# The last feed-forward block's second product as seven half-size products, with the residual transposed into the banks of two accumulators

## The chip, the cores and the metric

One NeuronCore of one Trainium2 chip runs the whole kernel in one launch. The time is that of the device, in microseconds, as the median of several executions. The engines are called PE (TensorE, with PEld for its weight loads), DVE (VectorE), ACT (ScalarE), POOL (GpSimd) and SP (SyncE, which here only issues transfers).

## What is computed

The reference is a decoder of two layers on x, float32, 2 x 2048 rows of 512: attention, cross attention, a feed-forward part of three residual blocks, then a long convolution, another cross attention and a mixture of experts. The change is in the feed-forward part, which for each of three blocks does this on the normalised x, with weights dequantised from integers:

```
h = x
for blk in range(3):
    i0, i1 = (2 * blk, 2 * blk + 1)
    y = _qlora_linear(h, qweights[i0], scales[i0], biases[i0], lora_a[i0], lora_b[i0])
    y = _layernorm(y, ln_gamma[blk], ln_beta[blk])
    y = jax.nn.gelu(y, approximate=False)
    y = _qlora_linear(y, qweights[i1], scales[i1], biases[i1], lora_a[i1], lora_b[i1])
    h = y + h
return h
```

and then adds the result to the x that came in.

## The kernel before, in words

The feed-forward stage (stage_ffn, L1240 to L1967) keeps h transposed in on-chip memory (hT, four tiles of 128 features by all 4096 rows). Rows are worked in chunks of 512 (eight chunks, NC; four tiles of 128 rows each, TJ). A step s is one chunk of one block, 24 in all; LAST is 16, the first step of the last block. A step has two units for the first product (FIRST) and two for the second, one unit for the row tiles tb and tb+2. The list `units` sets the order on PE and DVE: first product of step s+1, then second product of step s.

First products, and the second products of blocks 0 and 1 (SECOND), are Strassen-Winograd products: seven products of half size (`product`, L1810 to L1813: two matmuls of 128x256 each) in place of eight. Each needs sums of tiles: of rows (mix_rows on POOL, L1466 to L1480), of the hidden tiles after gelu (mix_hidden on POOL, L1482 to L1496), and of the weights (mix_first and mix_second on DVE). A unit uses three banks, a, b and e, in the order p1, p4 of the unit before, p2, p5, p6, p3, p7 (`fast`); DVE takes the results out piece by piece between them (`evict`, L1666 to L1692; c21 of a unit comes in the evict of the next one, after its first piece).

The second product of the last block (WHOLE) is done in full: for each tile of 128 rows four matmuls of 128x512 (L1945), and four of 128x128 with the identity as moving operand that add the transposed hT, the residual, into the same bank (L1947). DVE adds the bank to a tile of xn (L1703). That tile was filled by `base` on POOL (L1498 to L1505): x plus the last bias.

Queues around this. POOL's program, for each step s: mix_hidden(s) (only for s < LAST), rstd2 of step s+1, mix_rows of step s+2, and base of output chunk s+2-LAST. base(c+2) waits for the load of x (L1430) and for the store of chunk c (L1417), since it fills the same half of xn. SP's program, for each output chunk c: wait for the last eviction of the chunk, issue its store, in chunk 5 issue the early loads of the next stage (L1980 and L1981), then issue the load of x for chunk c+2. The last chunk is stored tile by tile (L1422). ACT turns the hidden tiles through gelu into gT (L1757) and normalises y (L1741); PE turns y for it (turn_g, L1799), for step s+1 inside the first unit of step s+2.

Of the kernel before, what the change touches and what calls it, by code (L numbers as in the profile page):

```python
# [1239 lines left out]
def stage_ffn(nc, st, nxt, x_in, x_out, bias, gamma, beta):  # L1240
# [7 lines left out]
    with st:  # L1248
# [50 lines left out]
        o_mm = st.sem("o_mm")  # L1299
        o_done = st.sem("o_done")  # L1300
# [4 lines left out]
        FIRST, SECOND, WHOLE = range(3)  # L1305
# [11 lines left out]
        fast_before = [sum(k != WHOLE for k, _, _ in units[:g]) for g in range(len(units) + 1)]  # L1317
        nth = lambda kind, s, tb: fast_before[unit_at[kind, s, tb]] + 1
# [3 lines left out]
        whole_part = lambda s, u: (s - LAST) * TJ + u + 1  # L1322
# [42 lines left out]
        def chunk_set(s):  # L1365

            n = nth(SECOND, s, 1)
            return [(c11_done, n), (c12_done, n), (c22_done, n), (c21_done, n)]

        @block.sync  # L1370
        def _(sp):
# [40 lines left out]
            for c in range(NC):  # L1412
                s = LAST + c
                if c < NC - 1:
                    sp.wait_ge(o_done, whole_part(s, TJ - 1))
                    st.plain(sp)
                    sp.dma_start(chunk_rows(x_out, c), xn[:, c % 2]).then_inc(stored[c % 2], 16)  # L1417
                else:
                    for u in range(TJ):
                        sp.wait_ge(o_done, whole_part(s, u))  # L1420
                        st.plain(sp)
# [13 lines left out]
        def _(pool):  # L1435
# [46 lines left out]
            def mix_hidden(s):  # L1482
# [28 lines left out]
            for s in range(-1, NS):  # L1511
                if 0 <= s < LAST:
# [17 lines left out]
        def _(dve):  # L1530
# [40 lines left out]

            def mix_second(b):
# [27 lines left out]
            def work(g, slot):  # L1600

                kind, s, tb = units[g]
                if kind == FIRST:
# [17 lines left out]
                    if tb == 1 and slot == 2:  # L1621
# [3 lines left out]
                        if s - 1 == NC:  # L1625
                            mix_second(1)
                else:
# [17 lines left out]
            def places(g):  # L1645

                kind, s, tb = units[g]
                if kind == FIRST:
                    return [y[:, tb + 2 * r, half_] for r in range(2) for half_ in (lo, hi)]
                first = rows(s).start  # L1650
                return [hT[:, tb + 2 * r, first + h * HW:first + (h + 1) * HW] for r in range(2) for h in range(2)]

            def plus_bias(g, dst, bank, right, lower):

                kind, s, tb = units[g]
                if kind == FIRST:
                    return dve.tensor_tensor(dst, bank, b0[:, s // NC, hi if right else lo], ALU.add)
                u = tb + 2 * lower
                return dve.scalar_tensor_tensor(dst, bank, b1c[:, s // NC, u:u + 1], dst, ALU.add, ALU.add)

            def c21(g):
                dve.wait_ge(p4_mm, fast_before[g] + 1)
                plus_bias(g, places(g)[2], ps[:, g % 2, 0:HW], 0, 1).then_inc(c21_done, 1)

            def evict(g):
                kind, s, tb = units[g]  # L1666
                n = fast_before[g] + 1
# [1918 lines left out]
```

## Time and profile before

| what | us |
|---|---|
| median of 3 runs | 5355.99 |
| all runs | 5347.31, 5355.99, 5356.1 |
| the profiled execution, its own time | 5345.93 |
| span of its first to last instruction | 5344.1 |
| the last block's second products, from 1611.95 to 1843.30 | 231.35 |
| mean granted TensorE clock, share of full | 0.98 |

In a timeline each row gives the start, how long it took, engine, line, operation, and what is written from what; x4 means that four instructions are merged. A float32 matmul is recorded as two. Matmul ends are modelled, so the time that a group costs PE is read from the distance between starts. What stands in brackets is idle time of the engine before it and what ended it.

### The profile page before, as it was taken

What the parts mean: (1) busy time and instruction counts of PE and PEld (TensorE: products, weight loads), DVE (VectorE), ACT (ScalarE), POOL (GpSimd) and SP (SyncE); (2) the same over time, 40 slices, a digit from 0 to 9 for tenths busy, and PEclk for the clock granted to TensorE, in tenths of its full rate; (3) what the DMA queues carried; (4) which work ended last, traced back from release to release, by engine and by line L of the source; (5) the groups of instructions that cost most, each with busy time, mean ns of one, the idle gap of its engine ahead of it and who ended that gap; (6) DMA issues with size and microseconds to landing.
All of it is one profiled execution on the core that took longest, in us unless ns stands there. A gap on an engine that the chain in (4) does not pass through costs nothing. (4 is left out here: it accounts for less than half of the span.)

```text
span 5344.1 us, 79687 instructions
## 1 busy us (share of the span) xinstructions
PE 5070.8 (95%) x26624; PEld 2763.8 (52%) x26624; DVE 2764.3 (52%) x4714; ACT 1732.0 (32%) x2238; POOL 1691.6 (32%) x1428
## 2 busy tenths in 40 slices
PE   9999989979999999899979999699999999999998
PEld 4444446668887566444444555534444444444444
DVE  4243237756663355355532565555555555555554
ACT  1011015534332200334321433134444444444433
POOL 1000005545553211000012222534444444444443
PEclk9999999989999999999999999899999999999999
DMA  1010021230012233799976022335546667889996
GB/s 58 8 48 8 11 83 53 65 97 32 24 32 63 101 107 132 171 219 216 221 198 226 24 72 77 100 105 150 179 143 189 211 216 250 267 288 332 383 383 235
DMA packets 493432, 771.88 MB, mean 144 GB/s; under 512 B 119505, under 2 KB 263638, under 8 KB 492708
## 3 DMA queue, kind: packets, MB, share of 16 engines
q1 hardware_dynamic: 377072, 723.32, 41.9%
q0 software_dynamic: 36160, 43.09, 4.1%
q10 hardware_dynamic: 79988, 2.67, 1.0%
q8 instruction: 129, 2.11, 0.2%
q14 instruction: 83, 0.68, 0.0%
HBM read 577.15 MB, written 116.26 MB: 130 GB/s over the span
## 5 line engine op out<-in xcount | busy, mean ns | idle before, releaser
L3467 PE MATMUL ex_ps<-ex_w,ex_xT 128*64 128x512 f32 x5248 | 1192.9, 596 | 13.3 <-DVE ex_w L3369 11.7
L3369 DVE COPY ex_w<-ex_shelf 128x4096 f32 x328 | 753.2, 2296 | 368.0 <-PE ex_ps L3467 243.4
L3418 ACT ACTIVATE ex_w<-ex_shelf 128x4096 f32 x164 | 593.4, 3618 | 888.3 <-PE ex_ps L3483 770.1
L3467 PEld LDWEIGHTS ex_ps<-ex_w,ex_xT 128*64 128x64 f32 x5248 | 366.4, 137 | 625.8 <-issue 589.0
L3483 PE MATMUL ex_ps<-ex_w,ex_hT 128*64 128x256 f32 x5248 | 596.8, 380 | 26.0 <-issue 22.1
L3315 POOL DMA_INDIRECT ex_x<-moe_xn,ex_ix x328 | 558.1, 1702 | 132.4 <-issue 99.0
L3332 POOL DMA_INDIRECT out<-ex_y,ex_ix_out x164 | 293.6, 1790 | 894.5 <-DVE ex_xT L3356 432.0
L3483 PEld LDWEIGHTS ex_ps<-ex_w,ex_hT 128*64 128x64 f32 x5248 | 383.9, 137 | 283.2 <-issue 119.7
L2759 POOL TENSOR_TENSOR go_xb<-go_xr,go_bias 128x2048 f32<-128x2048 f32 x8 | 38.2, 4775 | 719.0 <-DMA go_xr<-x 652.8
L3375 DVE TENSOR_TENSOR ex_h<-ex_g,ex_ps 128x512 f32<-128x512 f32 x164 | 112.5, 686 | 252.1 <-PE ex_ps L3467 214.3
L617 PE MATMUL at_ps<-at_xT,at_kT 128*128 128x512 f32 (+3 forms) x640 | 239.3, 529 | 1.6 <-ACT at_kT L511 1.6
L617 PEld LDWEIGHTS at_ps<-at_xT,at_kT 128*128 128x128 f32 x640 | 116.7, 190 | 121.8 <-issue 109.1
L1757 ACT ACTIVATE ff_gT<-ff_ps,ff_bet,ff_gam 128x128 f32<-128x128 f32 x384 | 137.5, 484 | 121.7 <-PE ff_ps L1799 121.6
L3423 ACT ACTIVATE ex_g<-ex_ps 128x512 f32<-128x512 f32 x164 | 98.0, 597 | 232.8 <-issue 232.8
L2624 PE MATMUL cv_ps<-cv_xin,cv_split 128*128 128x512 f32 x320 | 155.9, 626 | 17.7 <-ACT cv_g L2513 9.4
L2645 PE MATMUL cv_ps<-cv_gt,cv_fwd 128*64 128x256 f32 x1280 | 157.0, 388 | 9.3 <-DMA cv_gt<-cv_g 9.3
L1741 ACT ACTIVATE ff_y<-ff_y,ff_nm,ff_rs 128x512 f32<-128x512 f32 x96 | 72.8, 807 | 272.2 <-POOL ff_nm L1461 272.2
L2580 DVE TENSOR_TENSOR cv_m<-cv_z,cv_hat 128x512 f32<-128x512 f32 x128 | 79.8, 685 | 150.0 <-ACT cv_z L2538 149.5
L891 POOL TENSOR_TENSOR xb_s<-xb_s,xb_rec 128x616 f32<-128x616 f32 x64 | 78.0, 1218 | 233.1 <-DVE xb_rec L961 232.1
L575 PE MATMUL at_ps<-at_v,at_low 128*128 128x512 f32 x336 | 146.8, 592 | 0.0
L2513 ACT ACTIVATE cv_g<-cv_ps 128x512 f32<-128x512 f32 x160 | 94.7, 599 | 136.8 <-PE cv_ps L2624 136.7
L2191 PE MATMUL pr_ps<-pr_t,pr_s 128*128 128x384 f32 x384 | 135.9, 487 | 3.2 <-DVE pr_t L2114 1.4
(360 smaller groups left out, 8130.6 us busy)
## 6 DMA issues: line engine op xcount, KB each, us to landing
ex_shelf<-L_ffn_w SPq DMA_DIRECT2D x128, 2048.0 KB, 17.0
ex_shelf<-L_ffn_wo SPq DMA_DIRECT2D x64, 2048.0 KB
cv_gt<-cv_g SPq DMA_DIRECT2D x320, 128.0 KB, 3.7
cv_vt<-cv_v SPq DMA_DIRECT2D x256, 128.0 KB, 5.2
ff_x<-x SPq DMA_DIRECT2D x16, 1024.0 KB, 7.5
ex_raw_x<-slot_token ACTq DMA_DIRECT2D x656, 0.5 KB
at_low<-x SPq DMA_DIRECT2D x8, 1024.0 KB, 8.4
x<-at_acc SPq DMA_DIRECT2D x8, 1024.0 KB, 4.2
```

Source lines behind the costliest of these rows:

```text
L575: i = pe.matmul(ps[:, 4 + n % 4, :], prob[g][:, j % 4, (it - 4 * g) * P:(it - 4 * g + 1) * P], v[:, j, :], start=j == js[0], stop=j == js[-1])
L617: i = pe.matmul(ps[:, bank + ic - origin // CH, lo - ic * CH:], kT[:, k, j * P:(j + 1) * P], xT[:, k, lo:(ic + 1) * CH], start=k == 0, sto ...
L1757: i = act.activation(gT[:, k, j * P:(j + 1) * P], ps[:, side_bank(("g", s, j)), k * P:(k + 1) * P], ACT.Gelu, bias=bet[:, b, k:k + 1], sca ...
L2191: i = pe.matmul(bank[:, 0:NPC], lhs[:, k], rhs[:, k], start=first and k == 0, stop=k == HK - 1, skip_group_check=not first)
L2624: i = pe.matmul(bank, split[:, u // 4, :], rows, start=True, stop=True)
L2645: i = pe.matmul(ps[o * RT:(o + 1) * RT, z_bank(n, q) + ri, u * CW:(u + 1) * CW], fwd[:, r, ri, :], gt[:, n % 2, r, :], start=True, stop=True)
L3315: pool.indirect_dma_start(out=x[:, p, h, :], out_offset=None, in_=xn_q, in_offset=bass.IndirectOffsetOnAxis(ap=ix[:, p, h:h + 1], axis=0)) ...
L3332: pool.indirect_dma_start(out=out_q, out_offset=bass.IndirectOffsetOnAxis(ap=ix_out[:, p:p + 1], axis=0), in_=y[:, p, :], in_offset=None, ...
L3369: dve.tensor_copy(w_s[n][:, :], pick(shelf[n], buf)).then_inc(w_set[n].sem, 1)
L3418: act.activation(w_s[2][:, :], pick(shelf[2], buf), ACT.Copy).then_inc(w_set[2].sem, 1)
L3467: mm = pe.matmul(ps[q * G:(q + 1) * G, which, 0:FQ], xT[:, p % 2, k, :], wu[which][:, k, q * FQ:(q + 1) * FQ], start=k == 0, stop=k == KD - 1)
L3483: mm = pe.matmul(ps[q * G:(q + 1) * G, 4, 0:DQ], hT[:, p % 2, k, :], wd[:, k, q * DQ:(q + 1) * DQ], start=k == 0, stop=k == FC - 1)
```

## The change

The units of the last block are of a new kind, THIRD, and run through `fast` and `evict` as the others do. WHOLE, its two functions and the semaphores o_mm and o_done go away, and so does the case distinction of three helpers that told when a bank is free. In place of weights as the stationary operand, gT is (the result has rows on the partitions). The diff, cut to its core:

```diff
-            units += [(SECOND if s < LAST else WHOLE, s, tb) for tb in range(2)]
+            units += [(SECOND if s < LAST else THIRD, s, tb) for tb in range(2)]
...
+        second = lambda s: SECOND if s < LAST else THIRD
...
-        def chunk_set(s):
+        def chunk_set(s, tb=1):
...
-            n = nth(SECOND, s, 1)
+            n = nth(second(s), s, tb)
             return [(c11_done, n), (c12_done, n), (c22_done, n), (c21_done, n)]
...
                 if c < NC - 1:
-                    sp.wait_ge(o_done, whole_part(s, TJ - 1))
-                    st.plain(sp)
+                    for done in chunk_set(s):
+                        sp.wait_ge(*done)
+                        st.plain(sp)
                     sp.dma_start(chunk_rows(x_out, c), xn[:, c % 2]).then_inc(stored[c % 2], 16)
                 else:
-                    for u in range(TJ):
+                    for u in TILES:
+                        for done in chunk_set(s, u % 2):
...
                 if s:
-                    pool.wait_ge(p4_mm, nth(SECOND, s - 1, 1))
+                    pool.wait_ge(p4_mm, nth(second(s - 1), s - 1, 1))
                 g11, g12, g21, g22 = gT[:, 0:HK, lo], gT[:, 0:HK, hi], gT[:, HK:KD, lo], gT[:, HK:KD, hi]
+                if s >= LAST:
+                    g21, g12 = g12, g21
+                    pool.tensor_tensor(g_t[:, X3], g11, g21, ALU.subtract).then_inc(g_t_done, 1)
+                    pool.wait_ge(g_t_done, n + 1)
+                    pool.tensor_tensor(g21, g21, g22, ALU.add).then_inc(g_t_done, 1)
+                    pool.wait_ge(g_t_done, n + 2)
+                    pool.tensor_tensor(g_t[:, X2], g21, g11, ALU.subtract).then_inc(g_t_done, 1)
+                    pool.wait_ge(g_t_done, n + 3)
+                    pool.tensor_tensor(g_t[:, X4], g12, g_t[:, X2], ALU.subtract).then_inc(g_t_done, 1)
+                    return
...
             for s in range(-1, NS):
-                if 0 <= s < LAST:
+                if s >= 0:
                     mix_hidden(s)
...
+            def mix_third():
+                b = NB - 1
+                v = w[:, b % 2, 1]
+                b11, b12, b21, b22 = v[:, 0:HK, lo], v[:, 0:HK, hi], v[:, HK:KD, lo], v[:, HK:KD, hi]
+                dve.wait_ge(w_done, KD * 2 * NB)
+                dve.wait_ge(p4_mm, nth(SECOND, LAST - 1, 1))
+                dve.tensor_tensor(w_s[:, X3], b22, b12, ALU.subtract).then_inc(w_s_done, 1)
...
                         if s - 1 == NC:
                             mix_second(1)
+                        if s - 1 == LAST:
+                            mix_third()
...
             def c21(g):
-                dve.wait_ge(p4_mm, fast_before[g] + 1)
+                dve.wait_ge(p4_mm, g + 1)
+                if units[g][0] == THIRD:
+                    dve.wait_ge(c11_done, g + 1)
                 plus_bias(g, places(g)[2], ps[:, g % 2, 0:HW], 0, 1).then_inc(c21_done, 1)
...
+                if kind == THIRD and tb == 0:
+                    dve.wait_ge(base_done, s - LAST + 1)
                 plus_bias(g, d11, a, 0, 0).then_inc(c11_set, 1)
-                if g and units[g - 1][0] != WHOLE:
+                if g:
                     c21(g - 1)
                 work(g, 0)
                 dve.wait_ge(p2_mm, n)
                 dve.wait_ge(c11_set, n)
-                dve.tensor_tensor(d11, b, d11, ALU.add).then_inc(c11_done, 1)
+                if kind == THIRD:
+                    both = xn[:, s % 2, tb::2, lo]
+                    dve.tensor_tensor(both, ps[:, 2 + g % 2, :].rearrange("p (r d) -> p r d", r=2), both, ALU.add).then_inc(c11_done, 1)
+                else:
+                    dve.tensor_tensor(d11, b, d11, ALU.add).then_inc(c11_done, 1)
...
+                if kind == THIRD:
+                    dve.wait_ge(c22_set, n)
+                    both = xn[:, s % 2, tb::2, hi]
+                    dve.tensor_tensor(both, ps[:, 4 + g % 2, :].rearrange("p (r d) -> p r d", r=2), both, ALU.add).then_inc(c12_done, 1)
+                    dve.wait_ge(c12_done, n)
...
-            def evict_whole(g):
...
+                if kind == THIRD:
+                    return {1: (gT[:, 0:HK, mine], v[:, 0:HK, lo]), 2: (gT[:, HK:KD, mine], v[:, HK:KD, lo]), 4: (gT[:, HK:KD, next_], w_s[:, X4]),
+                            5: (gT[:, 0:HK, next_], v[:, 0:HK, hi]), 6: (g_t[:, X2, :, mine], w_s[:, X2]),
+                            3: (g_t[:, X4, :, mine], v[:, HK:KD, hi]), 7: (g_t[:, X3, :, mine], w_s[:, X3])}
...
+            def residual(g, k, bank):
+
+                _, s, tb = units[g]
+                for q in range(TJ):
+                    i = pe.matmul(bank[:, q * P:(q + 1) * P], hT[:, k + q % HK, rows(s, tb + q // HK * 2)], ident[:, :],
+                                  start=q >= HK, stop=True, skip_group_check=True)
+                return i
...
-                if g and units[g - 1][0] != WHOLE:
+                if g and units[g] != (THIRD, NS - 1, 0):
                     p4(g - 1)
                 side_work(g, 0)
-                bank_b_free(g)
-                product(bb, *op[2], True).then_inc(p2_mm, 1)
-                bank_e_free(g)
+                if g >= 2:
+                    pe.wait_ge(c11_done, g - 1)
+                last = product(bb, *op[2], True)
+                if kind == THIRD:
+                    last = residual(g, 0, bb)
+                last.then_inc(p2_mm, 1)
...
                 side_work(g, 2)
                 if kind == FIRST:
                     pe.wait_ge(h_s_done, 4 * (2 * s + tb) + 3)
+                elif kind == THIRD and tb == 0:
+                    pe.wait_ge(g_t_done, 4 * s + 4)
                 pe.wait_ge(c22_set, n)
-                product(eb, *op[3], False).then_inc(p3_mm, 1)
+                last = product(eb, *op[3], False)
+                if kind == THIRD:
+                    last = residual(g, HK, eb)
+                last.then_inc(p3_mm, 1)
...
-            def whole(g):
...
-                if units[g][:2] == (WHOLE, NS - 1) and units[g][2] == 0:
+                if units[g] == (THIRD, NS - 1, 0):
+                    p4(g - 1)
                     for j in TILES:
                         turn_g(NS - 1, j)
-                if units[g][0] == WHOLE:
-                    whole(g)
-                else:
-                    fast(g)
+                fast(g)
+            p4(len(units) - 1)
```

Unchanged in `fast`, and reached by the new units: ahead of p5 the first unit of a step waits for the second operation of mix_hidden (g_t_done 4s+2), ahead of p6 for the third.

## Rows read from the trace of the kernel before

**Rows 1.** The page's first part: busy time of each engine.

```profile
PE 5070.8 (95%) x26624; PEld 2763.8 (52%) x26624; DVE 2764.3 (52%) x4714; ACT 1732.0 (32%) x2238; POOL 1691.6 (32%) x1428
```

**Rows 2.** Stretches: us, busy of PE, PEld, DVE, ACT, POOL, clock, DMA share, GB/s.

```profile
1611.95:1843.30 231.35, 226.57 (x965) 153.04 (x963) 77.64 (x173) 61.09 (x140) 80.66 (x110) 0.99 0.21 68
1661.27:1692.42 31.15, 31.15 (x139) 21.77 (x138) 11.51 (x26) 8.73 (x20) 12.99 (x18) 1.00 0.22 68
```

**Rows 3.** Timeline of PE, a second product of the last block and what follows.

```profile
1674.25 3.60 PE L1945 MATMUL ff_ps<-ff_w,ff_gT 128*128 128x512 f32 x8
1677.68 1.05 PE L1947 MATMUL ff_ps<-ff_ident,ff_hT 128*128 128x128 f32 x8
1678.57 1.03 PE L1812 MATMUL ff_ps<-ff_w_t,ff_hT 128*128 128x256 f32 x4
1679.44 3.60 PE L1945 MATMUL ff_ps<-ff_w,ff_gT 128*128 128x512 f32 x8
...
1691.53 1.05 PE L1947 MATMUL ff_ps<-ff_ident,ff_hT 128*128 128x128 f32 x8
1692.42 1.03 PE L1812 MATMUL ff_ps<-ff_w,ff_hT 128*128 128x256 f32 x4
```

**Rows 4.** Timeline, weight loads beside their matmuls, and a DVE eviction.

```profile
1701.73 0.84 PEld L1812 LDWEIGHTS ff_ps<-ff_w,ff_h_s 128*128 128x128 f32 x4
1701.94 1.03 PE L1812 MATMUL ff_ps<-ff_w,ff_h_s 128*128 128x256 f32 x4
...
1702.22 0.41 DVE L1679 TENSOR_TENSOR ff_y<-ff_ps,ff_y 128x256 f32<-128x256 f32 x1
```

**Rows 5.** Timeline of block 1 around the start of a first product.

```profile
1569.65 1.03 PE L1812 MATMUL ff_ps<-ff_w,ff_hT 128*128 128x256 f32 x4
...
1571.38 1.04 PE L1799 MATMUL ff_ps<-ff_ident,ff_y 128*128 128x128 f32 x8
...
1572.43 0.47 DVE L1659 SCALAR_TENSOR_TENSOR ff_hT<-ff_ps,ff_b1c,ff_hT 128x256 f32<-128x256 f32 x1
...
1577.78 1.27 POOL L1490 TENSOR_TENSOR ff_g_t<-ff_gT 128x512 f32<-128x512 f32 x1 [0.68 <-ACT ff_gT L1757]
...
1581.83 1.27 POOL L1496 TENSOR_TENSOR ff_g_t<-ff_gT,ff_g_t 128x512 f32<-128x512 f32 x1
```

**Rows 6.** Timelines of SP and POOL, last block: store, x load, base, twice.

```profile
1693.40 0.38 SPq L1417 DMA_DIRECT2D x<-ff_xn  x1
...
1693.88 0.44 SPq L1430 DMA_DIRECT2D ff_x<-x  x1
...
1702.07 4.52 POOL L1505 TENSOR_TENSOR ff_xn<-ff_x,ff_b 128x2048 f32<-128x2048 f32 x1 [8.62 <-DMA ff_x<-x]
...
1789.01 1.14 SPq L1430 DMA_DIRECT2D ff_x<-x  x1
...
1799.55 4.51 POOL L1505 TENSOR_TENSOR ff_xn<-ff_x,ff_b 128x2048 f32<-128x2048 f32 x1 [12.66 <-DMA ff_x<-x]
```

**Rows 7.** Timeline of PE in block 1, where DVE mixes its second weights.

```profile
1390.72 1.03 PE L1812 MATMUL ff_ps<-ff_gT,ff_w 128*128 128x256 f32 x4
...
1395.12 1.10 PE L1812 MATMUL ff_ps<-ff_gT,ff_w 128*128 128x256 f32 x4 [1.65 <-DVE ff_w_s L1584]
...
1397.07 1.13 PE L1812 MATMUL ff_ps<-ff_gT,ff_w_s 128*128 128x256 f32 x4
```

**Rows 8.** Timeline of the end of the stage, the last chunk.

```profile
1817.01 1.04 PE L1799 MATMUL ff_ps<-ff_ident,ff_y 128*128 128x128 f32 x8
...
1817.64 5.69 ACT L1757 ACTIVATE ff_gT<-ff_ps,ff_bet,ff_gam 128x128 f32<-128x128 f32 x16 [4.28 <-PE ff_ps L1799]
...
1823.39 5.35 PE L1945 MATMUL ff_ps<-ff_w,ff_gT 128*128 128x512 f32 x8 [2.07 <-ACT ff_gT L1757]
...
1842.65 0.69 DVE L1703 TENSOR_TENSOR ff_xn<-ff_ps,ff_xn 128x512 f32<-128x512 f32 x1 [3.64 <-PE ff_ps L1947]
```

**Rows 9.** The four microseconds inside that slow restart.

```profile
1825.00:1829.00 4.00, 4.00 (x11) 1.86 (x10) 0.00 (x0) 0.00 (x0) 0.00 (x0) 0.78 0.00 0
```

More of the change, by code:

```diff
@@ L1314, in stage_ffn @@
                 units += [(FIRST, s + 1, tb) for tb in range(2)]
-            units += [(SECOND if s < LAST else WHOLE, s, tb) for tb in range(2)]
+            units += [(SECOND if s < LAST else THIRD, s, tb) for tb in range(2)]
         unit_at = {u: g for g, u in enumerate(units)}
-        fast_before = [sum(k != WHOLE for k, _, _ in units[:g]) for g in range(len(units) + 1)]
-        nth = lambda kind, s, tb: fast_before[unit_at[kind, s, tb]] + 1
+        nth = lambda kind, s, tb: unit_at[kind, s, tb] + 1
+        second = lambda s: SECOND if s < LAST else THIRD
         part = lambda s, u: s * TJ + u + 1
         seq = lambda s, j: s * TJ + TILES.index(j) + 1
-        whole_part = lambda s, u: (s - LAST) * TJ + u + 1
         QUARTERS = [(b, i, k) for b in range(NB) for i in range(2) for k in range(KD)]
@@ L1649, in places @@
                     return [y[:, tb + 2 * r, half_] for r in range(2) for half_ in (lo, hi)]
+                if kind == THIRD:
+                    return [xn[:, s % 2, tb + 2 * r, half_] for r in range(2) for half_ in (lo, hi)]
                 first = rows(s).start
@@ L1657, in plus_bias @@
                     return dve.tensor_tensor(dst, bank, b0[:, s // NC, hi if right else lo], ALU.add)
+                if kind == THIRD:
+                    return dve.tensor_tensor(dst, bank, dst, ALU.add)
                 u = tb + 2 * lower
@@ L1687, in evict @@
                 dve.wait_ge(c12_set, n)
[L1688 removed]
+                if kind == THIRD:
[3 more added lines that the diff above has]
+                    dve.wait_ge(c12_done, n)
+                else:
+                    dve.tensor_tensor(d12, e, d12, ALU.add).then_inc(c12_done, 1)
                 dve.wait_ge(p7_mm, n)
@@ L1692, in evict @@
                 work(g, 2)
-            def evict_whole(g):
-                _, s, tb = units[g]
-                c = s - LAST
-                for i in range(2):
-                    u = 2 * tb + i
-                    dve.wait_ge(o_mm, whole_part(s, u))
-                    if u == 0:
-                        dve.wait_ge(base_done, c + 1)
-                    o = xn[:, c % 2, u, :]
-                    dve.tensor_tensor(o, ps[:, 2 * i + g % 2, :], o, ALU.add).then_inc(o_done, 1)
-                    if i == 0 and units[g - 1][0] != WHOLE:
-                        c21(g - 1)
-                    work(g, 2 * i)
             for j in range(TJ):
@@ L1720, in _ @@
             for g in range(len(units)):
-                if units[g][0] == WHOLE:
-                    evict_whole(g)
-                else:
-                    evict(g)
+                evict(g)
+            c21(len(units) - 1)
         @block.scalar
@@ L1931, in fast @@
                 product(ab, *op[7], False).then_inc(p7_mm, 1)
-            def whole(g):
-                _, s, tb = units[g]
-                b = s // NC
-                if tb == 0:
-                    pe.wait_ge(g_done, part(s, TJ - 1))
-                    if s % NC == 0:
-                        pe.wait_ge(w_done, KD * (2 * b + 2))
-                for i in range(2):
-                    u = 2 * tb + i
-                    bank = ps[:, 2 * i + g % 2, :]
-                    (bank_b_free if i else bank_a_free)(g)
-                    for k in range(KD):
-                        pe.matmul(bank, gT[:, k, u * P:(u + 1) * P], w[:, b % 2, 1, k, :], start=k == 0, stop=False)
-                    for k in range(KD):
-                        o = pe.matmul(bank[:, k * P:(k + 1) * P], hT[:, k, rows(s, u)], ident[:, :], start=False, stop=k == KD - 1)
-                    o.then_inc(o_mm, 1)
-                    if i == 0:
-                        if units[g - 1][0] != WHOLE:
-                            p4(g - 1)
-                        side_work(g, 0)
             for n in range(KD):
```

59 lines of the change are left out of this document (21 added, 38 removed).

## The prediction, made before any run of the changed kernel

> **What bounds the kernel now.** I read the page's busy line first: PE is busy 95% of the span, every other engine about half or less [rows 1]. The stretches come next. From the start of the last block's second products to their end, 231.35 us, PE is busy 226.57 of them, and in one whole chunk of 31.15 us it has no gap at all, while POOL is busy 12.99 and DVE 11.51 [rows 2]. So in this stage time is the number of passes that PE makes, and another engine counts only where PE waits for it.
>
> The timeline of PE gives the prices, as spacing of starts, since ends are modelled and overlap [rows 3]. A matmul of float32 is two records. Four matmuls of 128x512 last from 1674.25 to 1677.68, 3.435 us; the four 128x128 ones that add the residual 0.89; a half-size product (two of 128x256) 0.865. A tile of the old second product is thus 4.325 us, a chunk 17.3 us and 0.865 for the fourth product of the unit before, which sits in it. The first product's two units take 12.98, the 31.15 of a chunk less the 18.17 from 1674.25 to 1692.42.
>
> **PE's work.** Removed per chunk: 4 x 3.435 = 13.74 us. Added: 14 products x 0.865 = 12.11. The residual stays: four groups of four 128x128 matmuls, 4 x 0.89, since each of two accumulators takes the halves of two tiles. Net 1.63 us a chunk, 8 chunks: **-13.0 us**, if nothing waits. The p4 of a chunk's last unit moves 0.865 into the next chunk's first unit, which makes that pair 13.84 us long.
> In the trace the weight loads lie under the matmuls: four loads of 0.84 us in sum stand beside products that still follow each other every 0.865 us [rows 4]. So the greater number of loads is free.
> The Trainium skill (TensorE: Matmul & The Clock Gate, Part 3) says that a weight load overlaps running matmuls only where it targets another row group of the array; here all 128 rows are used, so by that rule the 24 added loads of a chunk, 107 ns each by its section on LDWEIGHTS, would cost 2.6 us, more than the gain. The trace contradicts it.
>
> **Evictions.** Two DVE operations of 128x512 per unit (0.69 us; a row of them comes with the tail) become two of that size and five of 128x256, 0.41 to 0.42 each [rows 4]; with the statistics some 5 us in a unit of 7.83. The last residual matmuls end 0.865 before p7, so the widened eviction is done before c22 can start, and c22 is done 1.5 us after those matmuls, where PE wants it at 2 x 0.865 = 1.73. Nothing, if PE is not late already; if DVE were more than 0.2 us slower, p4 would wait by the rest.
>
> **Where POOL puts the new mixing: the term that decides.** The mixing of the hidden tiles is four operations on POOL, 1.35 us apart, the last ending 5.32 after the first begins [rows 5]. It now runs in the last block too. POOL's program has, for chunk s: mixing, row statistics, row mixing, and then the base of output chunk s+2. That base is queued ahead of the next mixing. It waits for an x load, which SP issues behind the store of chunk s, which waits for that chunk's last eviction. In the trace, with T the start of the next first product (1692.42): store issued T+0.98, load T+1.46, base T+9.65 to T+14.17 [rows 6]. Today that costs nothing, as the base is wanted a chunk later.
> After the change the last eviction is the c21 behind p4. In block 1, where this order runs already, it starts at T+2.78 (T is 1569.65) behind the turns of the hidden tile [rows 5]; it ends near T+3.2, so store, load and base all come 2.3 us later. The base then runs from T+12.0 to T+16.5, and the mixing from T+16.5: second operation done at T+19.1, third T+20.5, fourth T+21.8.
> PE reaches the second product at T+13.84, and p5, which wants the second operation, at T+13.84 + 3 x 0.865 + 0.89 = T+17.3; p3, which wants the fourth, would start at T+19.05 and starts at T+21.97 with 0.15 us for the semaphore. **Stall 2.9 us**, in five chunks: **+14.6**.
> In the sixth chunk the next stage's early loads are between store and load: load at T+3.15, base at T+13.69, with T at 1692.42 + 3 x 31.15 [rows 6]. Moved by 2.3, the mixing starts at T+20.5 and p3 waits for T+26.0: **+7.0**, and PE, idle near 6 us ahead of p5, is likely to go on at the lower clock: +0.7 that the waits don't cover. Bounds for one stall: DMA is busy 0.22 of a chunk [rows 2], 6.9 us for store and load together, against the 8.7 from the store's issue to the base; at best the base comes 1.8 us sooner and the stall is 1.1. If each load took the 10.5 us of the sixth, it is 5.3. I take 2.9, since store and load stay the same pair, 0.48 us apart, on the same queue.
>
> **Mixing the last weights.** DVE does it at the place of block 1's mixing. There p3 came 6.35 us after p1 [rows 7] instead of 5 x 0.865; the residual covers 0.89 of these 2.03, the wider eviction adds 0.28: **+1.4** (bounds 0.5 and 2.1).
>
> **The tail.** Before the last turns, p4 waits for c22 of the unit just ended, 0.75 us; after the last p7 the same again, then c21. Between them, gelu takes 5.69 us and PE restarts slowly: 5.35 us for what is 3.60 elsewhere [rows 8], at a granted clock of 0.78 over four us, partly at the lower of its levels, 1.2 GHz against 2.4 [rows 9]. The mixing's 5.32 us lie under the first five products and the residual at that pace (p3 wanted at 13.5 us after the old start of turns, reached near 14.0). From there to the last eviction 26.7 us against 26.3, with 1.63 already credited and 0.86 of p4 moved in: +1.2. Tile 1's store is now issued at the end too, by one more issue of 0.4 to 0.5: together **+1.7** (bounds 0.5 and 4).
>
> **Sum:** -13.0 + 14.6 + 7.0 + 0.7 + 1.4 + 1.7 = +12.4 us. The profiled execution took 5345.9, its span 5344.1; so 5358.3 for one like it. The median of the runs, 5356.0, is 10.1 above that execution (the runs lie at two levels, 5347 and 5356), and I forecast against it: 5356.0 + 12.4, rounded to **5368**. A difference under 0.2%, 10.7 us, is about what a measurement of this kernel can't tell from no change, and mine is just outside.
>
> **Rivals.** (A) The queue of POOL is not late: the base's load lands before T+9, the mixing ends by T+19 and no chunk stalls. For: DMA is idle most of a chunk, and POOL too. Against: the bases shown start 8.2 and 10.5 us after their loads' issue, ended by the load [rows 6], and the DMA share allows only 1.8 us of the 2.9 needed. It decides where the base starts more than 2.9 us sooner than my T+12.0. Then -13.0 + 1.4 + 1.7 = -9.9: 5346, not slower. Chance 0.08.
> (B) Half the stall, the load coming 1.5 us sooner or the store being released before the turn: -9.9 + 7.3 + 3.5 = +0.9: 5357. Chance 0.10.
> (C) The idle gaps also cost clock. After a gap of 2.07 us, with two before it, eight passes took 1.75 more [rows 8]; after 1.65 alone a product took 0.07 more [rows 7]. The new gaps, 2.0 and twice 0.45, lie between. If all five cost it, +8.8: 5377. Chance 0.14.
> (D) The loads are exposed. By rows, 24 more matmul records a chunk, each with a load of the 0.21 us that the four of rows 4 average, less what hides: half of it would be 2.5 us a chunk, 20 in all: 5388. Against: the spacing of starts shows nothing of it [rows 3, 4]. Chance 0.02. The rule of the Trainium skill given above (TensorE: Matmul & The Clock Gate, Part 3) would work this way.
> The forecast has 0.66; alone it spans 5360 to 5376.
>
> **How the numbers follow.** Range 5354 to 5382: it takes in B, C and the spread of the two levels, and leaves out A's 0.08, D and the ends of the rest. Slower by over 0.2%: not quite two thirds of the forecast's 0.66 (0.41), as its centre is only 1.7 us beyond that bound, and all of C and D: 0.57. Faster: half of A, as its -10 sits on the bound, and 0.01 of B: 0.05. Within: 0.38.
>
> **What the new profile would show.** PE: in the last block products 0.865 apart, 128x128 groups 0.89; a gap of about 2 us before p5 and two of 0.45, released by POOL's mixing, in chunks 17 to 21, about 6 us in the 22nd; none like it in chunk 16. A chunk of 32.4 us against 31.15. POOL: base, then the four mixing operations with no gap. SP: store at T+3.3. The forecast is wrong if POOL's mixing runs ahead of the base, if the base starts before T+10, if products space wider than 0.87, or if p4 waits for c22.

## The result, and the profile after

The changed kernel took **5367.81 us**, median of 11 runs (5360.93 to 5378.3), against 5353.94 for the kernel before in 11 runs beside it (5342.31 to 5362.15). The medians are 13.9 us apart. The ratio, taken over all runs, is 1.0031 [1.0023, 1.0038], some 16.6 us: slower, with the whole interval above the 0.2% under which the forecast took a difference for none. Forecast: 5368, from +12.4. The fit to 0.2 us is partly luck: the forecast added 12.4 to a median of before of 5356.0, 2 us above this one. And the two levels, 5347 and 5356, that it read from three runs of the kernel before are not there in more runs: these 11 are scattered over the whole of 5342 to 5362. The profiled execution took 5365.58 us, its span 5363.8.

The page's first part, after [rows 1]:

```profile
PE 5074.4 (95%) x26816; PEld 2810.6 (52%) x26816; DVE 2799.6 (52%) x4798; ACT 1731.4 (32%) x2238; POOL 1734.5 (32%) x1460
```

This line tells nothing of the cause. PE's share is 95% before and after, and PE even looks 3.6 us busier, although 12.9 us of passes were saved. In the last block its busy time did fall, by 2.8 us (below), so the rise comes from stages that the change doesn't touch; and the last block's fall is small because a matmul at the lower clock, or in front of a gap, is recorded as longer. The stretches tell more [rows 2]: the last block from its first second product to the next stage's first turn, then two of the running chunks, the sixth one, and the tail, from the end of the last chunk but one.

```profile
1610.33:1858.36 248.03, 223.77 (x1158) 192.39 (x1156) 111.78 (x257) 61.09 (x140) 117.08 (x139) 0.97 0.20 65
1627.49:1659.69 32.20, 30.32 (x162) 26.13 (x161) 15.43 (x37) 8.73 (x20) 18.02 (x21) 1.00 0.21 66
1659.69:1693.91 34.22, 31.73 (x161) 27.27 (x160) 15.43 (x37) 8.73 (x20) 18.01 (x21) 0.95 0.19 62
1790.74:1827.65 36.91, 32.08 (x161) 27.78 (x159) 15.43 (x37) 8.73 (x20) 13.69 (x16) 0.91 0.26 88
1827.65:1858.36 30.71, 22.52 (x110) 18.68 (x109) 7.80 (x17) 5.69 (x16) 5.10 (x5) 0.89 0.19 69
```

The same stretch was 233.25 us long before (1611.95 to 1845.20), so 14.8 of the 19.7 us between the two spans lie in it. Of the rest, the part ahead of it took 1.6 us less and the part behind it 6.5 more; that part takes from 3499 to 3516 us in the profiles of this document, whatever the edit. PE's busy time in the stretch fell from 226.57 to 223.77, and the time in which it stood idle rose from 233.25 - 226.57 = 6.7 to 248.03 - 223.77 = 24.3. A chunk that had no gap in 31.15 us now lasts 32.20 and has 1.9 us of gaps (gaps here are counted against modelled ends, and come out somewhat short). Chunk 17's second product in PE's timeline (T, the start of its first product, is 1627.49):

```profile
1641.33 1.03 PE L1836 MATMUL ff_ps<-ff_w,ff_gT 128*128 128x256 f32 x4
1642.19 1.03 PE L1836 MATMUL ff_ps<-ff_w_t,ff_hT 128*128 128x256 f32 x4
1643.06 1.03 PE L1836 MATMUL ff_ps<-ff_w,ff_gT 128*128 128x256 f32 x4
1643.92 1.05 PE L1868 MATMUL ff_ps<-ff_ident,ff_hT 128*128 128x128 f32 x8
1646.49 1.10 PE L1836 MATMUL ff_ps<-ff_w,ff_gT 128*128 128x256 f32 x4 [1.52 <-POOL ff_gT L1493]
1647.75 1.13 PE L1836 MATMUL ff_ps<-ff_w_s,ff_g_t 128*128 128x256 f32 x4 [0.15 <-POOL ff_g_t L1495]
1649.09 1.13 PE L1836 MATMUL ff_ps<-ff_w,ff_g_t 128*128 128x256 f32 x4 [0.21 <-POOL ff_g_t L1497]
1650.06 1.05 PE L1868 MATMUL ff_ps<-ff_ident,ff_hT 128*128 128x128 f32 x8
```

The products follow each other every 0.865 us and the residual takes 0.89, as before [rows 3]; then three products in a row wait, each for one operation of POOL's mixing. The bracket's number is idle time against modelled ends. Read the starts: from 1643.92 to 1646.49 are 2.57 us where the residual takes 0.89, then 1.26 and 1.34 where a product takes 0.865, together 2.55 us too much.

Who made POOL late stands in the timelines of DVE, SP and POOL for the same microseconds [rows 5, 6]:

```profile
1630.27 0.41 DVE L1686 TENSOR_TENSOR ff_xn<-ff_ps,ff_xn 128x256 f32<-128x256 f32 x1
```

```profile
1630.78 0.38 SPq L1415 DMA_DIRECT2D x<-ff_xn  x1
1631.27 0.43 SPq L1429 DMA_DIRECT2D ff_x<-x  x1
```

```profile
1639.26 4.52 POOL L1514 TENSOR_TENSOR ff_xn<-ff_x,ff_b 128x2048 f32<-128x2048 f32 x1 [10.16 <-DMA ff_x<-x]
1643.73 1.27 POOL L1491 TENSOR_TENSOR ff_g_t<-ff_gT 128x512 f32<-128x512 f32 x1
1645.09 1.26 POOL L1493 TENSOR_TENSOR ff_gT<-ff_gT 128x512 f32<-128x512 f32 x1
1646.43 1.27 POOL L1495 TENSOR_TENSOR ff_g_t<-ff_gT 128x512 f32<-128x512 f32 x1
1647.77 1.27 POOL L1497 TENSOR_TENSOR ff_g_t<-ff_gT,ff_g_t 128x512 f32<-128x512 f32 x1
```

The chain reads off from top to bottom: c21 ends at T+3.19, the store is issued at T+3.29, the x load at T+3.78, the base starts at T+11.8 and is followed by the four mixing operations with no gap. POOL had stood idle for 10.16 us in front of the base, waiting for the load, with the hidden tiles that the mixing reads ready at T+8.06, when gelu ended. This is a queue that is blocked at its head, not an engine that has too much to do.

All waits of PE over the six chunks and chunk 16's second product, by releaser (us in total, times, longest):

```profile
PE ff_ps L1836 <- POOL ff_gT L1493: 13.5, 6, 4.8
PE ff_ps L1836 <- POOL ff_g_t L1497: 0.9, 4, 0.2
PE ff_ps L1836 <- DVE ff_w_s L1593: 0.8, 1, 0.8
PE ff_ps L1836 <- DVE ff_xn L1734: 0.6, 1, 0.6
PE ff_ps L1836 <- DVE ff_xn L1686: 0.2, 1, 0.2
PE ff_ps L1836 <- POOL ff_g_t L1495: 0.2, 1, 0.2
```

Once per chunk POOL's second mixing operation, and the last weights' mixing once (L1593). The wait for c22 (L1734) comes only at the end of the stage, ahead of the last turns at 1828.39 and once more behind this window, at 1854.28, 0.57 us each; it comes in no running chunk.

The sixth chunk (T is 1790.74), in SP's, POOL's and PE's timelines [rows 6]:

```profile
1794.03 0.38 SPq L1415 DMA_DIRECT2D x<-ff_xn  x1
...
1796.14 1.20 SPq L1429 DMA_DIRECT2D ff_x<-x  x1
```

```profile
1805.84 4.51 POOL L1514 TENSOR_TENSOR ff_xn<-ff_x,ff_b 128x2048 f32<-128x2048 f32 x1 [13.49 <-DMA ff_x<-x]
```

```profile
1813.05 2.05 PE L1836 MATMUL ff_ps<-ff_w,ff_gT 128*128 128x256 f32 x4 [4.83 <-POOL ff_gT L1493]
1814.89 1.92 PE L1836 MATMUL ff_ps<-ff_w_s,ff_g_t 128*128 128x256 f32 x4
```

The base starts at T+15.1, PE waits 4.83 us and goes on at half speed: 1.84 us from p5's start to the next for what is 0.865, at a granted clock of 0.53 from 1813.05 to 1818.03, nearly all of it at 1.2 GHz of the two levels. And the tail [rows 8]:

```profile
1828.39 1.13 PE L1836 MATMUL ff_ps<-ff_w_s,ff_gT 128*128 128x256 f32 x4 [0.57 <-DVE ff_xn L1734]
1829.36 1.04 PE L1823 MATMUL ff_ps<-ff_ident,ff_y 128*128 128x128 f32 x8
...
1835.74 3.78 PE L1836 MATMUL ff_ps<-ff_w,ff_gT 128*128 128x256 f32 x8 [2.07 <-ACT ff_gT L1781]
1839.31 1.92 PE L1868 MATMUL ff_ps<-ff_ident,ff_hT 128*128 128x128 f32 x8
1841.02 1.33 PE L1836 MATMUL ff_ps<-ff_w,ff_gT 128*128 128x256 f32 x4
```

**The account of the 14.8 us:** chunk 16's second product -1.0 (18.17 to 17.16), six chunks +13.3 (6 x 31.15 = 186.9 to 200.2), the tail to the next stage's first turn +2.5 (28.19, from 1817.01 to 1845.20, to 30.71).

### The profile page after: what moved, and what is told of

The parts are those of the page before. It is cut to its first block and busy times, and to the rows that moved or that the text cites. A ratio compares the mean times of both kernels' runs of the same rounds, so it can differ in the third digit from the quotient of the medians.

```text
span 5363.8 us, 80325 instructions
## 1 busy us (share of the span) xinstructions
PE 5074.4 (95%) x26816; PEld 2810.6 (52%) x26816; DVE 2799.6 (52%) x4798; ACT 1731.4 (32%) x2238; POOL 1734.5 (32%) x1460
## 5 line engine op out<-in xcount | busy, mean ns | idle before, releaser
L3469 PE MATMUL ex_ps<-ex_w,ex_xT 128*64 128x512 f32 x5248 | 1194.8, 597 | 13.9 <-DVE ex_w L3371 11.4
```

Of the source, the lines that this page charges most:

```text
L3469: mm = pe.matmul(ps[q * G:(q + 1) * G, which, 0:FQ], xT[:, p % 2, k, :], wu[which][:, k, q * FQ:(q + 1) * FQ], start=k == 0, stop=k == KD - 1)
```

## The experiments

Theory: PE's saved passes are real, and the loss is made by the order of POOL's queue, base ahead of mixing, with the base waiting for a load that the late c21 has pushed back. Rivals: the pass saving itself isn't there (exposed loads, clock), or the stalls come from DMA or from DVE, whatever POOL's order. Two lengths are given for each run: the ratio to the kernel before, and **stretch B**, from PE's second turn of the last block's first chunk, near 1600 us, to the next stage's first turn. Before it is 244.95 us (1600.25 to 1845.20), after 259.73. It holds what the change touches, and it is free of the other stages' scatter: what lies outside it varied from 5099 to 5119 us over the profiles. It comes from one profile of each kernel, and the changed kernel alone gave 259.73 and 257.17, so a few us of it can be chance where the clock falls.

**The changed kernel again**, no edit.

> The changed kernel once more, as it is. Queue theory (POOL has the base of the next output chunk ahead of the hidden mixing, so PE waits for POOL): the same six gaps ahead of p5 in the last block, the first five 1.5 to 2.4 us, the sixth near 5; +12 to +16 us against the kernel before. Clock rival: the chunk that lost 2 us more (34.2 instead of 32.2, granted clock 0.95) is a matter of chance, so another chunk or none has it here; if it is the same chunk again with the same 12.6 us from the start of the first product to the base, the late load makes it.

Measured: 5369.92 us, ratio 1.0029 [1.0018, 1.004]; stretch B 257.17. By medians it is 17.1 us above the kernel before, by the ratio 15.5, and stretch B is 12.2 longer than before. The six gaps ahead of p5 came again: 1.61, 2.32, 1.53, 1.63 and the like, and 4.65 in the sixth. One chunk (18) again had a slower x load, 8.80 us from issue to base against 8.0 in the others, and again the longest of the five gaps, yet here without a lower clock behind it: 33.0 us where the first profile has 34.22.

**Base one chunk later.** POOL computes each base a chunk later in its program, when its load has long landed.

```
-                c = s + 2 - LAST
+                c = s + 1 - LAST
                 if 0 <= c < NC:
                     base(c)
```

> POOL makes the base of an output chunk one step later, behind the row mixing of that step, so the hidden mixing no longer stands behind a base that waits for a load. Queue theory: all six gaps go, a chunk takes 29.5 us instead of 32.2, and the kernel is 19 to 24 us faster than the changed one, 6 to 11 faster than the one before. Rival (the mixing of 5.3 us after gelu is itself too long, or the half-size products are not worth 1.63 us a chunk): gaps ahead of p5 or p3 remain, a chunk takes 31 us or more, and the time is at best that of the kernel before.

Measured: 5346.21 us, ratio 0.9988 [0.9978, 0.9997]; stretch B 236.34, so 23.4 us shorter than after and 8.6 shorter than before. POOL's timeline for the same chunk and PE's waits from 1600 to 1800 us:

```profile
1629.77 4.54 POOL L1514 TENSOR_TENSOR ff_xn<-ff_x,ff_b 128x2048 f32<-128x2048 f32 x1
1636.35 1.27 POOL L1491 TENSOR_TENSOR ff_g_t<-ff_gT 128x512 f32<-128x512 f32 x1 [2.04 <-ACT ff_gT L1781]
```

```profile
PE ff_ps L1836 <- DVE ff_w_s L1593: 0.8, 1, 0.8
PE ff_ps L1836 <- DVE ff_xn L1686: 0.2, 1, 0.2
```

```profile
1628.21:1657.75 29.54, 29.54 (x162) 26.11 (x161) 15.43 (x37) 8.74 (x20) 18.04 (x21) 1.00 0.23 72
```

The base has no bracket (it waits for nothing), the mixing starts when gelu is done, no wait for POOL is left, and the chunk is 29.54 us of busy PE: 1.61 less than before. The saving is all there; the queue took it and more.

**Load ahead of the store.** The other end of the same chain: SP issues the x load of a chunk before the store instead of behind it.

```
                 s = LAST + c
+                if c + 2 < NC:
+                    sp.wait_ge(base_done, c + 1)
+                    st.plain(sp)
+                    sp.dma_start(x[:, c % 2], chunk_rows(x_in, c + 2)).then_inc(...)
                 if c < NC - 1:
                     for done in chunk_set(s):
```

> POOL's order stays; SP issues the load of x for chunk c+2 ahead of the store of chunk c, so the base waits for the store alone. The store took 5.3 us from issue to landing, so the base starts near T+8.6 instead of T+11.8, and the mixing ends near T+18.5, before p3 wants it at T+19.05. Queue theory: the gaps go here too, within 2 us of the kernel with the later base. Rival (the base's place on POOL is enough to make PE late, whatever it waits for): the gaps stay at over half their size.

Measured: 5345.51 us, ratio 0.9985 [0.9976, 0.9993]; stretch B 236.37, the same as with the later base. The base now waits for the store, as was expected:

```profile
1637.66 4.53 POOL L1514 TENSOR_TENSOR ff_xn<-ff_x,ff_b 128x2048 f32<-128x2048 f32 x1 [7.29 <-DMA x<-ff_xn]
```

Its releaser is the store (`x<-ff_xn`), which has to have read the buffer that the base overwrites. T is 1628.77 here, so the base moved from T+11.8 to T+8.9, by 2.9 us, and the stall was 2.7: the fourth mixing operation ends at T+18.70, and p3 wants it at T+19.05, just in time. Chunks take 29.54 us here too, by the distance of the stores. Two ways to break one chain give the same length, which speaks for the chain and against a cost in POOL's work itself.

**c21 ahead of the next unit's first eviction.** On DVE, the last eviction of a chunk is taken before the next chunk's first one; POOL and SP stay as they are.

```
+                ahead = kind == FIRST and g > 0 and units[g - 1][0] == THIRD
+                if ahead:
+                    c21(g - 1)
                 dve.wait_ge(p1_mm, n)
...
                 plus_bias(g, d11, a, 0, 0).then_inc(c11_set, 1)
-                if g:
+                if g and not ahead:
                     c21(g - 1)
```

> After a unit of the last block DVE takes out its last piece (c21) ahead of the first piece of the next unit, so it doesn't wait for the turn of the hidden tile. The piece ends near T+2.4 instead of T+3.2, and if the chain c21, store, load, base, mixing, PE is one chain, each of the six gaps falls by 0.8 us: 4.9 us faster than the changed kernel, and a chunk takes 31.4 us. Rival (the load's landing is set by something else, or the gap by POOL's own length): no change of the gaps.

Measured: 5359.95 us, ratio 1.0016 [1.0007, 1.0025]; stretch B 251.17, 8.6 shorter than after. Chunk 31.41 us by the distance of two stores; gaps ahead of p5 of 0.73 to 0.91 where they were 1.5 to 2.3, and 3.61 in the sixth. PE's waits from 1600 to 1830 us:

```profile
PE ff_ps L1839 <- POOL ff_gT L1493: 7.7, 6, 3.6
```

The store is issued at T+2.45 instead of T+3.29, and four of the first five gaps shrink by 0.6 to 0.9 us: the c21 is the first link of the chain. But stretch B fell by 8.6 us, not by the 4.9 of the forecast. The chain's share is about 5.1: 0.6 to 0.9 in each of the first five chunks (chunk 18 taken as 0.8), and 1.2 in the sixth gap. The other 3.5 came besides. Chunk 18 lost a further 1.9 of its length, as its x load took 8.1 us this time, not 8.8, and the clock didn't fall behind its gap of 0.82; and the restarts at the lower clock were shorter, by 0.2 us in the sixth chunk and 1.4 in the tail.

**Control: the later base in the kernel before.** The same edit as in "Base one chunk later", on the old kernel.

> The kernel before the change, with nothing but POOL's base made one step later. There no hidden mixing stands behind the base in the last block, and the base is wanted a chunk later. Queue theory: no difference, and the stretch from the last block's second products to the next stage's first turn stays at 233 us. Rival (the base costs something by itself where it stands, and the later base is faster for that): 2 us or more faster.

Measured: 5352.84 us, ratio 0.9993 [0.9983, 1.0004]; stretch B 244.89 against 244.95. The order of POOL's queue cost the old kernel nothing, as the forecast had read from the trace. The edit gains only where the mixing stands behind the base.

**Early loads behind the x load.** For the sixth chunk alone: SP issues the next stage's loads behind the last x load, not ahead of it.

```
-                if c == NC - 3:
-                    sp.wait_ge(stored[0], 16)
-                    st.plain(sp)
-                    nxt.early(sp)
                 if c + 2 < NC:
                     ...
+                if c == NC - 3:
+                    sp.wait_ge(stored[0], 16)
+                    st.plain(sp)
+                    nxt.early(sp)
```

> The changed kernel with SP's early loads for the next stage issued behind the x load of chunk 7 instead of ahead of it. Queue theory: only the sixth gap changes, from 4.8 us (and a restart at the lower clock) to the 1.5 to 2.3 of the others, so the sixth chunk takes 32.2 us less the p4 that lies outside, near 31.5, instead of 36.9: 4 to 6 us faster than the changed kernel, the first five gaps as before. Rival (the last gap is long for another reason, the next stage's traffic or the end of POOL's list): it stays over 4 us.

Measured: 5364.51 us, ratio 1.0019 [1.0009, 1.0029]; stretch B 254.41, 5.3 shorter than after.

```profile
1813.56 1.10 PE L1836 MATMUL ff_ps<-ff_w,ff_gT 128*128 128x256 f32 x4 [1.55 <-POOL ff_gT L1493]
1814.82 1.13 PE L1836 MATMUL ff_ps<-ff_w_s,ff_g_t 128*128 128x256 f32 x4 [0.15 <-POOL ff_g_t L1495]
```

The sixth chunk is now one like the others, 32.20 us (1794.53 to 1826.73; the 31.5 of the forecast was too low) against 36.91, with their gap and with the granted clock at 1.00. Its extra was the two loads ahead in SP's queue; with the long gap the lower clock went too. Chunk 18 had its slow load again here, 8.80 us, and behind its gap of 2.33 us the clock was 0.62 over 4.48.

**The last weights' mixing, cut in four.** On top of the later base: DVE mixes the last block's weights one operation at each of four places of the first product that runs ahead of chunk 16's second, instead of all four in one place.

```
-            def mix_third():
+            def mix_third(n):
...
                 kind, s, tb = units[g]
+                if kind == FIRST and s - 1 == LAST:
+                    mix_third(2 * tb + slot // 2)
```

> The kernel with the later base, and the four DVE operations that mix the last weights spread one by one over the four working places of the first product's two units ahead, instead of all four at its end. If the 1.4 us that chunk 16 loses (gaps of 0.76 and 0.22 us and shorter ones) come from that block of 2.9 us on DVE, the gaps go and the stretch from the last block's second products to the next stage falls from 224.6 to 223.2 us. Rival (DVE has no room in those units, at 0.86 us a product): PE waits for DVE inside the two units of the first product, by 0.3 to 0.7 us each time, and as much is lost there as is won.

Measured: 5347.15 us, ratio 0.9988 [0.9978, 0.9999]; stretch B 236.64 against 236.34: no gain. The gaps of 0.8 and 0.2 in chunk 16's second product went, but new ones of 1.46 and 0.21 came a little earlier, waiting for a DVE eviction. Timelines of DVE and POOL:

```profile
1601.83 4.25 DVE L1591 TENSOR_TENSOR ff_w_s<-ff_w 128x512 f32<-128x512 f32 x1
1606.00 0.41 DVE L1714 TENSOR_TENSOR ff_y<-ff_ps,ff_y 128x256 f32<-128x256 f32 x1
```

```profile
1601.01 4.52 POOL L1514 TENSOR_TENSOR ff_xn<-ff_x,ff_b 128x2048 f32<-128x2048 f32 x1
```

An operation that takes 0.68 or 0.69 us alone took 4.25 and ended 0.55 us after POOL's base. The evictions queued behind it, and PE behind them.

**The same, clear of the base.** The operations are put at the places none, first, second, third and fourth together, so that none meets the base. This kernel also has the idle turns of the next experiment.

```
                 if kind == FIRST and s - 1 == LAST:
-                    mix_third(2 * tb + slot // 2)
+                    for n in ((), (0,), (1,), (2, 3))[2 * tb + slot // 2]:
+                        mix_third(n)
```

> The kernel with idle turns and spread mixing, with the first mixing operation moved behind POOL's base: none at the first working place, then one, one and two. In the run with the spread mixing the first operation took 4.25 us on DVE, from 1601.83 to 1606.08, while POOL's base ran from 1601.01 to 1605.53; the others took 0.7 to 1.1. If the base locks DVE's operation out, this one takes 0.7 to 1.1 us too, PE's gap of 1.46 us in that unit goes, and the stretch from the second turn of the step before to the next stage falls from 235.7 to between 233.8 and 234.5 us. Rival (the operation was slow because it is the first after the dequantising, or DVE has no room in those units): it stays over 2 us or PE gets gaps of the same sum elsewhere.

Measured: 5344.18 us, ratio 0.9982 [0.9973, 0.9991]; stretch B 234.35.

```profile
1607.79 1.42 DVE L1591 TENSOR_TENSOR ff_w_s<-ff_w 128x512 f32<-128x512 f32 x1
...
1609.80 1.09 DVE L1591 TENSOR_TENSOR ff_w<-ff_w 128x512 f32<-128x512 f32 x1
...
1614.63 0.68 DVE L1591 TENSOR_TENSOR ff_w_s<-ff_w 128x512 f32<-128x512 f32 x1
```

The first two still ran beside POOL's mixing operations and took 1.42 and 1.09, the first of them more than the 0.7 to 1.1 of the forecast; the third, clear of them, took 0.68. The stretch is inside the forecast's range. One gap of 0.56 is left where there were 0.8 and 0.2.

**Turns in the gelu gaps.** On top of the cut mixing (the first form): PE makes 8, 4 and 16 idle turns of the identity, into a bank that is free, in the gaps of the last chunk, where gelu keeps it waiting.

```
                     p4(g - 1)
-                    for j in TILES:
+                    pe.wait_ge(c12_done, g - 1)
+                    for j, more in zip(TILES, (0, 8, 4, 16)):
                         turn_g(NS - 1, j)
+                        turn_idle(pe, ps[:, 4 + g % 2], ident, more)
```

> The kernel with the spread mixing, and 28 idle turns of the identity (8, 4 and 16) on PE in the gaps of the last chunk, where it waits for gelu. Before them the last chunk's first products ran at the lower clock: 3.78 us for what takes 1.9. If idle turns count as work for the clock, the restart is at full speed and the last chunk is limited by POOL's mixing alone: 1.5 to 2 us less, of 30.5. If they don't count, nothing changes, or it is slower by up to 1 us where a turn still runs when gelu is done.

Measured: 5340.63 us (5334.4 to 5345.17), ratio 0.9978 [0.997, 0.9987]; stretch B 235.70. The restart in PE's timeline with the later base alone, and here:

```profile
1813.54 3.78 PE L1836 MATMUL ff_ps<-ff_w,ff_gT 128*128 128x256 f32 x8 [2.08 <-ACT ff_gT L1781]
```

```profile
1813.10 1.91 PE L121 MATMUL ff_ps<-ff_ident 128*128 128x128 f32 x16
1815.33 1.99 PE L1834 MATMUL ff_ps<-ff_w,ff_gT 128*128 128x256 f32 x8 [0.33 <-ACT ff_gT L1779]
...
1819.37 1.13 PE L1834 MATMUL ff_ps<-ff_w_s,ff_g_t 128*128 128x256 f32 x4 [0.16 <-POOL ff_g_t L1495]
1820.71 1.13 PE L1834 MATMUL ff_ps<-ff_w,ff_g_t 128*128 128x256 f32 x4 [0.21 <-POOL ff_g_t L1497]
```

The first eight records take 1.99 us in place of 3.78, with the granted clock at 1.00 over 1812 to 1818 where it was 0.50. From the restart to the next stage it is 20.80 us against 22.14: of the 1.8 gained at the restart some goes back to waits for POOL's mixing, which the slow restart had hidden, the last two rows. Against the kernel that it was built on, whose restart was a shorter one, stretch B is 0.9 shorter: less than the 1.5 to 2 of the forecast.

**Later base and turns alone**, without touching the weights' mixing.

> The kernel with the later base and the idle turns, without the spread mixing. The two parts lie in different places, so they add: 236.3 us for the stretch with the later base alone, less the 1.34 us from the last restart on, gives 235.0 us. Rival (the 1.34 came with the spread mixing): it stays at 236.3.

Measured: 5345.71 us, ratio 0.9984 [0.9973, 0.9994]; stretch B 235.00, 1.3 less than with the later base alone.

**Which is best.** Six versions have medians under both kernels', and under the kernel before by 5 to 12 us. Only one of them (mixing cut, turns) is more than 0.2% below the kernel before; for the others the intervals end just under 1, up to 0.9999, and stretch B is the better evidence: 8.3 to 10.6 us shorter than before in all six. Their medians, 5340.63 to 5347.15, have overlapping intervals and don't rank them. Stretch B, of one profile each, is 244.95 before and 236.34 (later base), 236.37 (load first), 236.64 (mixing cut), 235.70 (mixing cut, turns), 235.00 (turns alone) and 234.35 (turns, mixing clear of the base).

## Why the prediction was right, and where its terms were off

**Products and weight loads.** Right. The products stand 0.865 apart and the residual takes 0.89; a chunk without stalls is 29.54 against 31.15, 1.61 where 1.63 was worked out, 12.9 over eight. Rival D is refuted: 29.54 us are filled by the passes alone at the old spacing, so nothing of the added loads is exposed. The sentence of the Trainium skill (TensorE: Matmul & The Clock Gate, Part 3) that weight loads overlap only where the row group differs doesn't hold here; the same Part also names a background weight buffer as a way for a load to run ahead, which the prediction left out and which would fit these rows.

**Evictions.** Right: no running chunk waits for c22; it waits at the end of the stage, where foreseen.

**POOL's order, five stalls.** Right in mechanism and nearly in size. Store T+3.29 for T+3.3, base T+11.8 for T+12.0, p5 at T+19.0 behind a gap, p3 at T+21.6 for T+21.97. A chunk is 32.20 for 32.4, a stall of 2.7 for 2.9. By the distances of the stores the five chunks took 32.20, 34.22, 32.23, 32.17 and 32.43, in sum 163.25 against 5 x 29.54 = 147.7: **+15.6 for 14.6**. Four cost 2.6 to 2.9 each; the excess is chunk 18, 4.7 us, where the load was slow by 0.8 and the clock fell behind the gap. Rivals A and B stand refuted for this kernel. A's condition, a base more than 2.9 us sooner than T+12.0, is just what the load ahead of the store brought about (T+8.9), and then the median is 7.3 us under the kernel before and stretch B 8.6 shorter; A had 9.9, with the tail's term too small by about one.

**Rival C** got something. Behind a gap of 2.34 us the clock was 0.61 over the next 4.4, worth about 1.2 us; behind 2.32 in the second profile nothing was lost; the gaps near 1.5 cost nothing in either. C asked for all five chunks and got one, in some executions only.

**The sixth chunk.** Right: 36.91 - 29.54 = 7.4 for 7.0 + 0.7. The base came at T+15.1, 0.9 sooner than the T+16.0 of the working, so the wait itself cost 6.0 for 7.0; the lower clock cost 1.4 for 0.7 (5.87 us from p5's start to p7's, against 4.46 in chunk 17). In the second profile the lower clock cost 0.6.

**The last weights' mixing.** Right: chunk 16's second product is 1.46 us longer than one that waits for nothing (17.16 against 29.54 - 13.84 = 15.70), for a forecast of 1.4. The gap is 0.76 and a second one of 0.22 follows.

**The tail was mis-sized.** The step that failed is "From there to the last eviction 26.7 us against 26.3". By the forecast's own terms the tail to the next stage's first turn should have grown by 0.9 us; it grew by 2.5. From 1827.65, where the turns stood in the old order, to the end of the last c21 it took 28.2 us. Most of it is in PE's rows of the restart: 3.57 us for the first eight records, then 1.71 for the residual's 0.89 and 1.17 for a product, at a granted clock of 0.56 over 6.76 us, where the old kernel was back at full spacing sooner [rows 8, 9]. That is a loss of 3.0 us, for the 1.75 of the old restart that the working had taken over. The other 0.4 or so is not the clock's: 0.1 lies ahead of the restart, and the time from the last eviction to the next stage's first turn grew by 0.6 where 0.4 to 0.5 was allowed. Set against the working, the term is 3.3, not 1.7.

How long the restart stays slow is not set by the order of work alone. With the same instructions in the tail it lost 3.0, 2.6, 2.5, 2.5, 2.1, 1.8 and 1.6 us in the seven profiles without idle turns, behind the same gap of 2.07 or 2.08 in all but one; the old order lost 1.75 and 1.70 in its two. This is the restart with the early loads behind the x load, where the residual is already at its full spacing:

```profile
1834.84 3.68 PE L1836 MATMUL ff_ps<-ff_w,ff_gT 128*128 128x256 f32 x8 [2.07 <-ACT ff_gT L1781]
1838.36 1.05 PE L1868 MATMUL ff_ps<-ff_ident,ff_hT 128*128 128x128 f32 x8
```

So the 1.75 was one draw of something that varies; the profile of the changed kernel drew the longest, and the tail grew by 1.1 to 2.5 us over these profiles. The idle turns confirm that the clock is the cost: with the clock kept, 1.3 us came back. What decides how long it stays down, the runs don't show.

In sum: -12.9 + 15.6 + 7.4 + 1.5 + 3.3 = +14.9 for the +14.8 of the profiles, and +12.4 in the forecast. About 1.2 us of the 15.6, 1.4 of the 7.4 and 3.0 of the tail's restart are the lower clock's, and vary from one execution to the next. The sign and the verdict hung on one reading, that the base of chunk s+2 stands ahead of the mixing in POOL's program and waits on SP's store; four edits at three links of that chain (POOL's order, SP's order twice, DVE's order) each gave back what the link was worth, the last of them with 3.5 us more that are not the chain's.

## What to carry to other kernels

When work is moved onto an engine that is two thirds idle, don't ask whether it has time but what stands ahead of it in that engine's program, and what that waits for: here a 4.5 us operation with a chunk of slack waited for a load behind a store behind an eviction, and everything queued after it lost its slack as well. Write down each point of the chain as an offset from the start of the chunk, compare it with the point at which the consumer wants it, and do so for the odd chunk too, where other loads slip in. An operation with slack belongs behind those without; that is one line of code, and worth about 22 us here against the changed kernel, though only 7 to 9 against the kernel before.

## What the runs showed of the hardware that was not expected

**DVE stands while POOL's base runs.** A subtraction of two SBUF operands took 4.25 us instead of 0.69 beside a 4.52 us POOL operation, and ended 0.55 us after it; moved behind the base, such an operation took 1.42 and 1.09 beside shorter POOL operations, and 0.68 with POOL idle. POOL's own mixing operations took 1.60 instead of 1.27 beside it. DVE's evictions, which read PSUM, stayed near 0.42 beside the base. The Trainium skill (SBUF — State Buffer, section SBUF: two separate sides) says that DVE and GpSimd share a port pair with an exclusive lock, held for the whole instruction by whichever starts first, and that a DVE operation needs it against a GpSimd operation that reads SBUF when both its inputs are in SBUF. The trace agrees: each of the three slowed subtractions ended 0.54 or 0.55 us after the POOL operation that it had met, and the evictions, with one input in PSUM, were not slowed.

**Turns keep the clock.** With 28 idle turns of the identity in float32 in the gaps, the granted clock was 1.00 over the restart in all three profiles. Without them it was 0.50, the lower level, over the first 3.57 us with the later base alone, and the restart was slow in every profile.

**Gaps of the same length, with and without a fall.** Behind gaps of 2.34 and 2.33 us the granted clock fell (0.61 and 0.62 over the next 4.4 to 4.5 us), and behind one of 2.32 it stayed at 1.00. The x load of chunk 18 took 8.8 us in all three of these profiles, 0.8 more than its neighbours, for a reason that the traces don't show; with c21 taken first it took 8.1.
